# Late q and k blocks turned by VectorE's shuffle, and squares, low halves and bias on GpSimd

## The reference

```
qkv = x @ w_qkv                        # 16 heads of 8
q, k = rmsnorm(q)*q_scale, rmsnorm(k)*k_scale
q, k = q*cos + rot(q)*sin, k*cos + rot(k)*sin      # rot swaps the halves of a head, one sign
attn = softmax(q*8**-0.5 @ k.T) @ v
x = layernorm(x + attn @ w_proj + b_proj)
h = silu(x@w1*s1) * (x@w2*s2)          # 128 -> 512
h = gelu(h@h1*s) ; h = gelu(h@h2*s)    # 512 -> 512, twice
x = layernorm(x + h@w3*s3)             # 512 -> 128
```

## Time and profile before

| | |
|---|---|
| median of 3 runs | 375.9 us (373.97 to 377.68) |
| profiled execution | 374.38 us |
| its span, first to last instruction | 372.7 us |
| mean granted clock of TensorE | 0.988 |
| first exponential of the first chunk, and of the second | 19.66 us, 92.96 us |

### The profile page before, as it was taken

How to read it: one execution, slowest core, us unless ns; L and a number is a source line. 1 busy time by engine, 2 the same in 40 slices (tenths; PEclk the granted TensorE clock), 3 DMA queues, 4 the chain that set the end, 5 groups by cost and what they waited for, 6 DMA issues and landing times.

```text
span 372.7 us, 6253 instructions
## 1 busy us (share of the span) xinstructions
PE 341.3 (92%) x2091; PEld 135.8 (36%) x2091; DVE 221.7 (59%) x465; ACT 304.7 (82%) x350; POOL 28.7 (8%) x41
## 2 busy tenths in 40 slices
PE   7878999998999989999999999999999899999980
PEld 2412223222322353443222545333223534435850
DVE  1997988866547715364466453545477153667753
ACT  2689999899999898789999897989998987854330
POOL 2023111102100000001100000011000000011001
PEclk9989999999999999999999999999999999999997
DMA  7909464426202110111111200202021100000001
GB/s 222 293 31 346 159 211 165 168 82 244 86 21 99 38 67 2 60 42 59 70 59 41 87 13 4 96 0 105 25 98 36 64 0 0 0 29 0 2 0 33
DMA packets 12295, 29.42 MB, mean 79 GB/s; under 512 B 1138, under 2 KB 4082, under 8 KB 12274
## 3 DMA queue, kind: packets, MB, share of 16 engines
q1 hardware_dynamic: 8368, 16.23, 12.9%
q0 software_dynamic: 3328, 12.06, 9.1%
q10 hardware_dynamic: 578, 0.85, 0.8%
HBM read 17.64 MB, written 9.44 MB: 73 GB/s over the span
## 4 chain that ended last, share of the span: by engine, by line
PE 63%; DVE 14%; ACT 10%; DMA 6%; issue 5%; POOL 1%; SPq 0%; POOLq 0%; DVEq 0%; ACTq 0%
PE ps L508 23%; PE ps L555 15%; PE ps L494 11%; ACT probs L843 8%; PE ps L545 4%; PE ps L663 4%; DMA va<-v_all 4%; DVE ffn L1060 2%; PE ps L461 2%; PE ps L625 2%; DMA xT<-in_x_t 1%; DMA k_scr<-parts 1%; DVE r L941 1%; PE ps L697 1%; PE ps L525 1%
## 5 line engine op out<-in xcount | busy, mean ns | idle before, releaser
L843 ACT ACTIVATE probs<-ps 128x1024 f32<-128x1024 f32 x256 | 242.6, 1035 | 24.8 <-PE ps L494 24.5
L508 PE MATMUL ps<-probs,va 128*9 128x512 f32 x896 | 112.7, 594 | 3.7 <-ACT probs L843 2.7
L494 PE MATMUL ps<-qa,ka 32*128 32x512 f32 x512 | 77.0, 499 | 8.2 <-ACT probs L843 6.0
L494 PEld LDWEIGHTS ps<-qa,ka 32*128 32x128 f32 x512 | 31.7, 183 | 105.6 <-ACT probs L843 60.3
L1060 DVE TENSOR_SCALAR ffn<-ps,col 128x512 f32<-128x512 f32 x36 | 27.0, 751 | 55.0 <-PE ps L555 50.8
L555 PE MATMUL ps<-g_hi,w_hi 128*128 128x512 f32 x108 | 45.5, 421 | 1.7 <-DVE ffn L1060 1.2
L555 PE MATMUL ps<-g_lo,w_hi 128*128 128x512 f32 x108 | 42.5, 393 | 0.0
L508 PEld LDWEIGHTS ps<-probs,va 128*9 128x9 f32 x896 | 15.8, 89 | 48.9 <-issue 27.3
L1035 DVE TENSOR_TENSOR g_lo<-ffn,g_hi 128x512 fp32r<-128x512 f32 x36 | 24.9, 692 | 1.2
L555 PEld LDWEIGHTS ps<-g_hi,w_hi 128*128 128x128 f32 x108 | 20.3, 188 | 14.5 <-DVE g_lo L1035 4.0
L439 POOL TENSOR_TENSOR rs<-ve,mhalf 128x4 f32<-128x4 f32 x6 | 6.1, 1022 | 227.5 <-DVE ve L1023 227.5
(11 more groups left out here) (129 smaller groups left out, 322.3 us busy)
## 6 DMA issues: line engine op xcount, KB each, us to landing
ka<-k_scr SPq DMA_DIRECT2D x14, 512.0 KB
k_scr<-parts POOLq DMA_DIRECT2D x8, 512.0 KB, 4.4
q_scr<-parts POOLq DMA_DIRECT2D x8, 512.0 KB, 5.1
qa<-q_scr SPq DMA_DIRECT2D x14, 256.0 KB
va<-v_all SPq DMA_DIRECT2D x14, 144.0 KB
ffn<-in_h POOLq DMA_DIRECT2D x1, 1024.0 KB, 6.1
h_raw<-in_h POOLq DMA_DIRECT2D x1, 1024.0 KB, 8.7
xT<-in_x_t SPq DMA_DIRECT2D x3, 256.0 KB, 6.6
```

What stands on the lines that cost most here:

```text
L494: mm = pe.matmul(s_tile(u)[:, i, :], ka[rows, slot, kt * P:(kt + 1) * P], qa[rows, slot, :], start=True, stop=not shifted)
L508: mm = pe.matmul(ps[32 * h:32 * h + VW, O_BANK, :], v, probs[:, step % 4, h, :], start=(kt == 0), stop=(kt == KT - 1))
L843: nc.scalar.activation(probs[:, step % 4, 2 * pair:2 * pair + 2, :], s_tile(u), ACT.Exp).then_inc(exp_done, 1)
```

## The change

- The swap tasks go. VectorE's shuffle, from the mix bank to SBUF, exchanges the half heads of every 8 partitions (`HALF_TURN`), and signals `late_raw`. The sine product is then made from SBUF in place (`late_turn`).
- The square is made by GpSimd from the shuffled copy (a head's squares have the same mean in either order). The cosine product no longer waits for the square, the sine product does. ScalarE's late squares go.
- The low halves of all weights and the bias add go to GpSimd, in between its stores and loads, each waiting for VectorE's high half (`w_high`). VectorE's largest low halves wait for `w_low`, the loop of later chunks for `bias_added`.
- The list has 13 tasks instead of 18, in other slots, and the later chunks count the mix bank's rounds from 13.

```diff
-MIX_FIRST = 18
+MIX_FIRST = 13
...
-TASK_SLOTS = (10, 18, 22, 23, 26, 30, 31, 34, 38, 40, 42, 46, 48, 50, 54, 56, 59, 62)
-SQUARE_PAIRS = (11, 23, 31, 43, 51)
-RINV_PAIRS = (22, 30, 38, 49, 57)
+TASKS = (("proj", 0), ("var", 0), ("proj", 1), ("var", 1), ("proj", 2), ("var", 2), ("v", 2),
+         ("proj", 3), ("var", 3), ("proj", 4), ("var", 4), ("v", 3), ("flag", 0))
+TASK_SLOTS = (10, 15, 18, 23, 27, 32, 35, 38, 43, 46, 51, 55, 61)
+RINV_PAIRS = (16, 24, 33, 44, 52)
+HALF_TURN = [m // HD * HD + (m + HD // 2) % HD for m in range(32)]
...
+            def low_part(raw, at, n, turn):
+                pool.wait_ge(w_high, turn)
+                pool.tensor_tensor(w_lo[:, at:at + n], raw, w_hi[:, at:at + n].bitcast(F32), ALU.subtract).then_inc(w_low, 1)
+            def low_half(raw, at, i, turn):
+                half = HM * HID // 2
+                low_part(raw[:, i * half:(i + 1) * half], at + i * half, half, turn)
+            def late_square(n):
+                pool.wait_ge(late_raw, n + 1)
+                raw = late_sets[n % 2][2]
+                pool.tensor_tensor(late_sets[n % 2][0], raw, raw, ALU.mult).then_inc(late_sq, 1)
             store(2, 1, 0)
-            pool.wait_ge(h1_taken, 1)
+            late_square(0)
+            low_half(h1_raw, H1, 0, 1)
+            low_half(h1_raw, H1, 1, 2)
+            pool.wait_ge(w_low, 2)
             stage(w_raw[:, W1:W1 + HID], w1, 1, in_w123)
             stage(w_raw[:, W2:W2 + HID], w2, 1, in_w123)
             stage(w_raw[:, 2 * HID:2 * HID + HM * P], w3, HM, in_w123)
+            low_half(h2_raw, H2, 0, 3)
+            late_square(1)
             store(3, 1, 1)
+            low_half(h2_raw, H2, 1, 4)
+            late_square(2)
             store(4, 2, 0)
+            pool.wait_ge(in_res, 64)
+            pool.tensor_tensor(xb[:], xb[:], bias_b[:, None, :].to_broadcast([P, NCH * TILES, P]), ALU.add).then_inc(bias_added, 1)
+            late_square(3)
             store(5, 2, 1)
+            low_part(w_raw[:, 0:2 * HID], W1, 2 * HID, 5)
+            low_part(w_raw[:, 2 * HID:2 * HID + HM * P], W3, HM * P, 6)
+            late_square(4)
             store(6, 3, 0)
...
             def late_products(n):
-                h = late_sets[n % 2][1]
-                mixed(0)
+                h, rot = late_sets[n % 2][1:]
+                k = mixed(0)
+                use[0] += 1
+                t, of = LATE[n]
+                nc.vector.stream_shuffle(rot, mix_bank, HALF_TURN).then_inc(late_raw, 1)
+                turned_by(mix_bank, of, t, h).then_inc(mix_free, 1)
+                dve.wait_ge(mix_free, k + 1)
+            def late_turn(n):
+                rot = late_sets[n % 2][2]
                 t, of = LATE[n]
                 dve.wait_ge(late_sq, n + 1)
-                turned_by(mix_bank, of, t, h).then_inc(mix_free, 1)
+                link(turned_by(rot, of + QS, t, rot), 0)
```

More of the change, by code:

```diff
@@ L233, in build @@
         q_out = [sem(f"q_out{t}") for t in range(NCH)]
-        h1_taken = sem("h1_stage_taken")
+        w_high = sem("w_high_written")
+        w_low = sem("w_low_written")
+        bias_added = sem("bias_added")
         aug_in = [sem("aug_in0"), sem("aug_in1")]
@@ L603, in first_task @@
                     pe.wait_ge(in_x[t], 16)
-                    mm = proj(of + (QS if kind == "swap" else 0), bank, t)
+                    mm = proj(of, bank, t)
                 mm.then_inc(mix_ready, 1)
@@ L821, in _ @@
             take_v(2, ps[:, 0, :])
[L823 to L827, removed]
             def late_inverse_root(n):
@@ L1159, in _, with high_part @@
             w_max = stats[:].rearrange("p t s -> p (t s)")
[L1161 to L1165, removed]
+            def high_part(raw, at, n):
+                nc.vector.tensor_copy(w_hi[:, at:at + n], raw).then_inc(w_high, 1)
             def largest_low(i, at, n):
@@ L1176, in first_chunk, with high_half @@
                 half = HM * HID // 2
-                def split_half(raw, at, i):
-                    return split_weights(raw[:, i * half:(i + 1) * half], at + i * half, half)
+                def high_half(raw, at, i):
+                    high_part(raw[:, i * half:(i + 1) * half], at + i * half, half)
                 late_products(0)
                 turn_group(0)
-                late_swap(0)
                 dve.wait_ge(in_h1, 16)
-                split_half(h1_raw, H1, 0)
-                split_half(h1_raw, H1, 1).then_inc(h1_taken, 1)
@@ L1187, in first_chunk @@
-                dve.wait_ge(in_h2, 16)
[L1188 to L1193, removed]
+                high_half(h1_raw, H1, 0)
+                high_half(h1_raw, H1, 1)
+                late_turn(0)
+                late_sum(0)
+                late_products(1)
@@ L1194, in first_chunk @@
+                dve.wait_ge(in_h2, 16)
+                high_half(h2_raw, H2, 0)
                 late_rows(0)
-                link(split_half(h2_raw, H2, 1), 0)
+                late_turn(1)
+                late_sum(1)
+                high_half(h2_raw, H2, 1)
                 late_products(2)
                 turn_group(1)
-                late_swap(2)
-                late_sum(1)
                 late_rows(1)
-                dve.wait_ge(h1_taken, 1)
+                late_turn(2)
+                late_sum(2)
@@ L1213, in first_chunk @@
-                late_products(4)
-                late_sum(3)
-                late_swap(4)
+                dve.wait_ge(in_w123, 48)
+                high_part(w_raw[:, 0:2 * HID], W1, 2 * HID)
+                high_part(w_raw[:, 2 * HID:2 * HID + HM * P], W3, HM * P)
+                late_turn(3)
+                late_sum(3)
+                late_products(4)
+                turn_group(2)
+                late_rows(3)
+                late_turn(4)
+                late_sum(4)
+                dve.wait_ge(w_low, 4)
@@ L1216, in first_chunk @@
+                largest_low(1, H2, HM * HID)
+                late_rows(4)
+                late_v(3)
+                dve.wait_ge(w_low, 5)
                 largest_low(2, W1, 2 * HID)
+                dve.wait_ge(w_low, 6)
                 link(largest_low(3, W3, HM * P), 0)
                 nc.vector.tensor_reduce(ve[:, 0:1], w_max[:, 0:4], AX.X, ALU.max).then_inc(w_split, 1)
-                late_rows(3)
-                late_sum(4)
-                late_rows(4)
-                late_v(3)
                 mixed(0)
@@ L1275, in _ @@
             start = links[0]
+            dve.wait_ge(bias_added, 1)
             with dve.Fori(1, NCH) as c:
```

23 lines of the change are left out of this document (3 added, 20 removed).

## The result

The changed kernel takes **402.64 us** (399.06 to 403.56, 4 runs) against 376.79 for the kernel before beside it (373.97 to 377.90): ratio 1.068, interval 1.062 to 1.073. Forecast was 389, range 380 to 399: the right side, too small by 13.6 us, outside the range. The profiled execution took 402.37 us with a span of 398.6.

What follows compares the result with a forecast made beforehand. ScalarE and TensorE in lockstep were taken to bound the first chunk. Terms -2.55 + 3.2 + 7.35 + 3.3 + 2.0 = +13.3 us; 374.4 + 13.3 + 1.5 = 389.2, so 389, range 380 to 399.

Steps and rivals of the forecast that it cites:

- rival of port contention: First chunk: VectorE's two-SBUF-input ops and GpSimd's arithmetic exclude each other for whole instructions; +3.2 and +4.7, 397 us, chance 0.35.
- variance 1: Slot 23, before pair 24: TensorE waits for square 1 behind GpSimd's low halves and loads; ScalarE idles 7.35 us.
- V of block 2: Slots 35 to 38, before pair 40: projection 3 waits for VectorE's late copies of V; ScalarE idles 3.3 us.
- Variance 0: Slot 15, before pair 16: TensorE waits for GpSimd's first square, behind shuffle and store 2; ScalarE idles 3.2 us.
- GpSimd's price: GpSimd's subtractions and squares estimated at 2.6 ns per column: 1.35 us a square, 2.7 a low half, 5.4 the bias.
- Clock: After TensorE's 6.7 us stand in the first chunk, a half clock lasts some 3.5 us, costing 2.0 us.
- odd slots: Slots 27, 35, 43, 51, 55: a task after the values idles ScalarE about 0.55 us each, 2.75 us together.
- The squares: First chunk, ScalarE: removing five squares of 0.48 us saves 2.4 us on the path.
- The swaps: First chunk, TensorE: removing five swap projections, 5.3 us, saves at most ScalarE's 2.9 us of waits.
- Outside the span: End of the sum: only 1.5 us added for median against profiled execution, no added cost from the change.
- Later chunks: After the first chunk: code unchanged, 79.0 us each as before, only shifted by 13.
- new bias wait: Start of the later chunks: waiting for GpSimd's bias add costs 0.0, as it is done at 75, over 25 us earlier.

Runs made afterwards that it cites:

- e1: Changed kernel with GpSimd's square of block 1 queued ahead of the third low half; 399.07 us, ratio 1.065.
- e3: Changed kernel with the bias add at the end of GpSimd's first-chunk queue and two memsets in its old place; 397.65 us, ratio 1.058.
- e4: Changed kernel with the low halves back on VectorE, squares and bias add still on GpSimd; 395.75 us, ratio 1.056.
- e15: Changed kernel with low halves on VectorE, bias add last on GpSimd, V of block 2 copied right after rows 1; 389.53 us, ratio 1.033.
- e5: Changed kernel with the squares back on ScalarE from the mix bank, low halves and bias add still on GpSimd; 398.38 us, ratio 1.059.
- e7: Kernel before, in its old slots, with the shuffle replacing the swaps and the squares on GpSimd; 378.07 us, ratio 1.008.
- e6: Kernel before, in its old slots, with only the shuffle replacing the swap projections; 378.49 us, ratio 1.003.
- e18: Kernel before with shuffle, squares on GpSimd, w1 to w3 loads later, and five empty mix-bank rounds in the swaps' slots; 378.34 us, ratio 1.008.

## Why the prediction was wrong in size

The step that failed is the one that kept VectorE's operations with two SBUF inputs at their 0.69 to 0.75 us beside GpSimd's arithmetic: the rival of port contention was set aside with 0.35, and that hold then lengthened the two terms "variance 1" (7.35) and "V of block 2" (3.3). By its own steps, on the profiled execution:

- **Variance 0**: forecast 3.2 us of idle, measured 3.28. Right in place, in size partly by luck: the square takes 1.04 instead of 1.35, but the variance ran at the half clock (2.02 instead of 1.06), which I had not granted to this stand. In e1, e3, e4 and e15, with the same code up to there, the idle was 4.1; in the changed kernel's execution ScalarE had idled 0.7 us more ahead of it than in those.
- **Variance 1**: forecast 7.35, measured 10.10. The place and one of two causes are right (e1: -3.6 by the queue alone). The term was mis-sized: GpSimd alone would have been earlier than I took it, but the low halves held VectorE's sine product and sum for 4.2 us, so its shuffle came at 50.4, where my prices give 44.2 (e4 and e5 show both parts).
- **V of block 2**: forecast 3.3 and "doesn't hang on GpSimd's price", measured 10.0. Here the failed step cost most. VectorE's order was late by itself: 4.8 with the bias moved (e3), 0.31 with the order mended (e15). The other 5 us were the bias add through the sum of block 2 (e3). The contention rival had just this place and 4.7 us, and I gave it 0.35.
- **The choice between the two.** Against contention I set that a subtraction beside GpSimd's DMA issue kept its 1.22. That row says nothing of the case, since no arithmetic of GpSimd is in it. The rule of the Trainium skill (SBUF — State Buffer, who interferes with whom) that I cited said exactly that it holds against ops that read, and I weighed it by a row without one.
- **Clock**: forecast one half-clock stretch, 2.0 us; there were three, of some 4, 10 and 10 us, the last two beginning within the stands. Idle beside the three gaps was 6.8 us, where I had 2.75 for the odd slots and 2.0 for the clock.
- **The squares** took 2.4 us off ScalarE, as forecast, but e7 has nothing of it in the span. **The swaps**, put at 2.9 at most: in e6 the whole part brought 1.2 us in the span, about its noise, since the rows of group 2 were next late. In the changed kernel, where I had written that they would not be, they held nobody, as TensorE stood elsewhere.
- **Outside the span**: 0 forecast, 2.2 measured. I had added 1.5 for median against profile, and taken the rest of an execution as fixed.
- **Later chunks** as before and the new bias wait at 0.0: right.

Idle together: forecast 3.2 + 7.35 + 3.3 + 2.75 + 2.0 = 18.6, measured 30.2. The contention rival's 397 was nearest; with the 2.2 outside the span and the 2.0 more of idle beside the three gaps it comes to 401, above a range that ended at 399.

## What to carry to other kernels

Work handed to GpSimd cost twice here: its own 2 to 2.3 ns per column in a queue where each item delays all behind it, and every VectorE operation with two SBUF inputs, or a cast, that met it (15.0 us held for 9.1 us taken off); so count it as taken from VectorE too, and look for who waits in order on either. Before a projection or a square is removed, look what lands next (here a load, for which TensorE then waited 2.0 to 3.3 us), for that bounds the gain. Where TensorE is left standing, count the half clock behind the stand as well; here each of the three had one.

## What the runs showed of the hardware that I had not expected

- A VectorE operation on one element with two SBUF inputs took 3.88 us beside a GpSimd add of 4.65 us, and one of 0.69 took 5.47 beside an add of 4.52. By the records it had begun 0.38 us before that add; yet a multiplication that began 0.16 us before a low half kept its 0.67, and there GpSimd was the one that waited (2.71 for 2.35).
- Behind a stretch of 2 us in which TensorE was still busy for 0.77 the granted clock was 0.50; I had counted a half clock only behind the longer stands.
- Time outside the span isn't a constant of the program's frame: 1.6 to 1.8 us with 18 rounds of the mix bank in the first chunk, 3.6 to 4.9 with 13, in every run of these kernels and of the kernel before beside them (only e18, with 18 rounds, lay at 1.8 to 2.3). Cause open.
